# Relation stage of a graph network kernel: the next matrix split over two chunks, rows copied ahead of the splits, half loads behind their own chunk's store

## The reference, cut to what matters

```python
seg = edge_type * n + dst                                  # 34 relations
agg = segment_sum(x[src], seg, num_segments=N_REL * n)
cnt = segment_sum(ones, seg, num_segments=N_REL * n)
mean = agg.reshape(N_REL, n, -1) / maximum(cnt, 1.0).reshape(N_REL, n, 1)
h1 = einsum('rni,rio->no', mean, W_rel) + x @ W_root + b_rgcn
```

## Time and profile before

| | |
|---|---|
| median of three runs | 2671.55 us (2663.07 to 2681.05) |
| span of the profiled execution, which is all that is given of its own time | 2698.0 us |
| PE busy | 2339.2 us (87%) |
| DVE busy | 1509.4 us (56%) |
| ACT busy | 1065.7 us (39%) |
| POOL busy | 955.5 us (35%) |
| relation stage, in the span | about 590 us to 1610 us |

### The profile page before, as it was taken

How to read it: one execution, slowest core, us unless ns; L and a number is a source line. 1 busy time by engine, 2 the same in 40 slices (tenths; PEclk the granted TensorE clock), 3 DMA queues, 4 the chain that set the end, 5 groups by cost and what they waited for, 6 DMA issues and landing times.

```text
span 2698.0 us, 50471 instructions
## 1 busy us (share of the span) xinstructions
PE 2339.2 (87%) x12981; PEld 2168.2 (80%) x13015; DVE 1509.4 (56%) x2625; ACT 1065.7 (39%) x1833; POOL 955.5 (35%) x1138
## 2 busy tenths in 40 slices
PE   3677798879999999999999996788698879978899
PEld 1355698869999999999999984567598879978899
DVE  6654478754444333443433337777636777678634
ACT  3211332323334333433433335555423355347421
POOL 4766100015565555555555547676300000000000
PEclk9999899989999999999999998999899989989999
DMA  6000105345555555565555547777602110011102
GB/s 218 7 0 0 44 11 219 117 157 192 183 196 179 189 194 171 186 196 185 180 181 194 184 152 253 238 229 218 212 12 81 37 42 0 12 47 58 59 12 104
DMA packets 121823, 347.21 MB, mean 129 GB/s; under 512 B 30391, under 2 KB 31371, under 8 KB 121717
## 3 DMA queue, kind: packets, MB, share of 16 engines
q1 hardware_dynamic: 79973, 219.37, 23.2%
q0 software_dynamic: 41808, 127.32, 16.1%
HBM read 258.18 MB, written 92.26 MB: 130 GB/s over the span
## 4 chain that ended last, share of the span: by engine, by line
PE 37%; DMA 19%; issue 18%; DVE 12%; SPq 6%; ACT 4%; DVEq 3%; POOL 1%; ACTq 1%; POOLq 0%; another core or an unknown queue 0%
PE ps L1585 17%; PE ps L1654 12%; DMA messages<-land 10%; DMA land<-in_L_gnn_W_rel 6%; PE ps L1720 4%; DMA land<-messages,stage 2%; PE ps L1576 2%; SPq L550 2%; PE ps L1794 1%; SPq L564 1%; DVE xw L1543 1%; DVE h_act L1154 1%; DVE land L1167 1%; DVE w_a L1065 1%; DVE land L1221 1%
## 5 line engine op out<-in xcount | busy, mean ns | idle before, releaser
L1585 PE MATMUL ps<-w_a,h_t 128*128 128x384 f32 x4968 | 921.2, 342 | 11.9 <-issue 7.3
L1585 PEld LDWEIGHTS ps<-w_a,h_t 128*128 128x128 f32 x4968 | 872.0, 191 | 24.3 <-issue 16.6
L1492 DVE TENSOR_TENSOR h_t<-ps,h_t 128x256 fp32r<-128x256 f32 x408 | 172.3, 423 | 583.7 <-ACT h_t L997 440.0
L1654 PE MATMUL ps<-xw,agg_w 128*128 128x384 f32 x2500 | 460.5, 344 | 35.9 <-DVE agg_w L1176 29.8
L1654 PEld LDWEIGHTS ps<-xw,agg_w 128*128 128x128 f32 x2500 | 447.9, 193 | 44.9 <-issue 39.1
L1585 PE MATMUL ps<-xw,h_t 128*128 128x384 f32 x2448 | 456.5, 343 | 2.2 <-DVE h_t L1492 2.0
L1585 PEld LDWEIGHTS ps<-xw,h_t 128*128 128x128 f32 x2448 | 432.8, 190 | 3.6 <-issue 3.4
L997 ACT ACTIVATE h_t<-ps 128x256 fp32r<-128x256 f32 x408 | 156.3, 384 | 536.0 <-PE ps L1585 354.5
L692 POOL DMA_INDIRECT stage<-slot_table,stage x171 | 180.2, 1054 | 211.0 <-DMA stage<-inv_table,stage 159.6
L1576 PE MATMUL ps<-ident,land 128*128 128x128 f32 x1176 | 167.2, 279 | 87.2 <-DVE land L1488 36.6
L786 POOL DMA_INDIRECT land<-messages,stage x184 | 213.4, 1160 | 81.0 <-issue 46.6
(11 more groups left out here) (226 smaller groups left out, 2238.1 us busy)
## 6 DMA issues: line engine op xcount, KB each, us to landing
land<-in_L_gnn_W_rel SPq DMA_DIRECT2D x198, 384.0 KB
messages<-land SPq DMA_DIRECT2D x136, 384.0 KB
land<-x_state SPq DMA_DIRECT2D x40, 384.0 KB, 3.1
messages<-land SPq DMA_DIRECT2D x9, 1536.0 KB, 17.0
land<-in_L_gnn_W SPq DMA_DIRECT2D x10, 1152.0 KB
x_state<-land SPq DMA_DIRECT2D x30, 384.0 KB, 2.3
adj<-x_state SPq DMA_DIRECT2D x10, 384.0 KB
h_act<-x_state SPq DMA_DIRECT2D x1, 3840.0 KB
```

The lines of the kernel that those rows point to most:

```text
L1492: dve.tensor_tensor(h_t[:, 1, 2 * g:2 * g + 2, :], turn_group(g).rearrange("p (k n) -> p k n", k=2), h_t[:, 0, 2 * g:2 * g + 2, :].bitcast ...
L1585: ins = pe.matmul(acc(h), h_t[:, a, k, :], w[:, b, k, h * HF:(h + 1) * HF], start=(k == 0 and a == 0 and b == 0), stop=(stop and k == KB - ...
L1654: ins = pe.matmul(ps[:, 2 + 2 * u + h, 0:wide], at, xw[:, c, b, h * HF:h * HF + wide], start=first, stop=last, skip_group_check=True)
```

## The change

Four things are edited in the relation stage.

1. SP: `next_matrix` becomes `next_half`, which loads the three blocks of one half, one after the other; each waits for the one before it. The first half stands behind the first chunk's store, the second half behind the second chunk's. Before the first relation both halves of matrix 1 are loaded in the same way.
2. ACT and DVE: three blocks of the next matrix are split in the first chunk and three in the second, one block after each high or low part. In `rel_out`'s place nothing changes but that the third block's split stands ahead of it.
3. DVE: `copy_rows` stands right behind the first `rel_low` of a chunk, in every chunk, ahead of the splits.
4. Each relation has at least three chunks instead of two. The largest number of chunks grows, and with it some index tables; `stage` and `ctl_low` are made smaller or moved.

```diff
-    CH = 2 * NR + (E - 1) // P
+    CH = 3 * NR + (E - 1) // P
...
-            def next_matrix(r, w):
-                sp.wait_ge(w_low, r * 2 + w_no["rel"] * 2)
+            def next_half(r, w, h):
+                sp.wait_ge(w_low, r * 2 + (w_no["rel"] * 2 - 1 + h))
                 sp.sem_inc(turn_taken, 1)
                 for k in range(3):
-                    for h in range(2):
-                        if k > 0:
-                            sp.wait_ge(w_land[h], r * 48 + (w_no["rel"] * 16 - 32 + k * 16))
-                            sp.sem_inc(turn_taken, 1)
-                        b = 3 * h + k
-                        sp.dma_start(w_raw[:, b:b + 1, :], w[:, b * P:(b + 1) * P, :].rearrange("a (k p) d -> p (a k) d", p=P))\
-                          .then_inc(w_land[h], 16)
+                    if k > 0:
+                        sp.wait_ge(w_land[h], r * 48 + (w_no["rel"] * 16 - 32 + k * 16))
+                        sp.sem_inc(turn_taken, 1)
+                    b = 3 * h + k
+                    sp.dma_start(w_raw[:, b:b + 1, :], w[:, b * P:(b + 1) * P, :].rearrange("a (k p) d -> p (a k) d", p=P))\
+                      .then_inc(w_land[h], 16)
...
-                store(c0, c0, base)
-                if w is not None:
-                    next_matrix(r + 2, w)
-                with sp.Fori(c0 + 1, c1) as c:
+                for h in range(2):
+                    store(c0 + h, c0, base)
+                    if w is not None:
+                        next_half(r + 2, w, h)
+                with sp.Fori(c0 + 2, c1) as c:
                     store(c, c0, base)
...
-                    for g in range(KG):
-                        rel_high(c0 + 1, g)
-                        if g < KG - 1:
-                            rel_split(r + 1, 1 - u, 2 * g)
-                    rel_out(c0)
-                    rel_split(r + 1, 1 - u, 4)
-                    with act.Fori(c0 + 1, c1) as c:
+                    for n in range(2):
+                        for g in range(KG):
+                            rel_high(c0 + (n + 1), g)
+                            rel_split(r + 1, 1 - u, KG * n + g)
+                        rel_out(c0 + n)
+                    with act.Fori(c0 + 2, c1) as c:
...
-                dve.tensor_scalar(size, size, 2.0, None, ALU.max).then_inc(K.dve, 1)
+                dve.tensor_scalar(size, size, 3.0, None, ALU.max).then_inc(K.dve, 1)
...
-                    for g in range(KG):
-                        rel_low(c0 + 1, g)
-                        if g < KG - 1:
-                            rel_split(r + 1, 1 - u, 2 * g)
-                    copy_rows(c0 + 2)
-                    rel_split(r + 1, 1 - u, 4)
-                    with dve.Fori(c0 + 1, c1) as c:
-                        for g in range(KG):
+                    for n in range(2):
+                        rel_low(c0 + (n + 1), 0)
+                        copy_rows(c0 + (n + 2))
+                        rel_split(r + 1, 1 - u, KG * n)
+                        for g in range(1, KG):
+                            rel_low(c0 + (n + 1), g)
+                            rel_split(r + 1, 1 - u, KG * n + g)
+                    with dve.Fori(c0 + 2, c1) as c:
+                        rel_low(c + 1, 0)
+                        copy_rows(c + 2)
+                        for g in range(1, KG):
                             rel_low(c + 1, g)
-                        copy_rows(c + 2)
```

More of the change, by code:

```diff
@@ L247, in gnn_stack @@
         edge_slot, edge_weight = keys[:, 0, :], keys[:, 1, :].bitcast(F32)
-        stage = sb("stage", [P, 32], I32)
+        stage = sb("stage", [P, 24], I32)
         chunk_pos = sb("chunk_pos", [1, CW], I32)
@@ L251, in gnn_stack @@
         ctl_rel = sb("ctl_rel", [1, NR + 2], I32)
-        ctl_half = sb("ctl_half", [1, 5], I32)
+        ctl_half = sb("ctl_half", [1, 6], I32)
         ctl_quad = sb("ctl_quad", [1, NT + 1], I32)
         ctl_col = sb("ctl_col", [1, NT], I32)
-        ctl_low = sb("ctl_low", [1, 1], I32)
+        ctl_low = ctl_half[:, 5:6]
         deg = sb("deg", [P, NT], F32)
@@ L569, in relation @@
                 base = sp.value_load(ctl_base[0:1, ds(r, 1)], min_val=0, max_val=E)
-                store(c0, c0, base)
-                if w is not None:
-                    next_matrix(r + 2, w)
-                with sp.Fori(c0 + 1, c1) as c:
+                for h in range(2):
[3 more added lines that the diff above has]
+                with sp.Fori(c0 + 2, c1) as c:
                     store(c, c0, base)
             sp.wait_ge(K.dve, K.ctl)
-            next_matrix(1, w_rel[1:2, :, :])
+            for h in range(2):
+                next_half(1, w_rel[1:2, :, :], h)
             with sp.Fori(0, NR - 2) as r:
@@ L980, in _, with rel_split @@
             act.wait_ge(G["L0b"].mm, 2 * G["L0b"].last)
[L982 to L986, removed]
+            def rel_split(r, slot, p):
+                act.wait_ge(w_land[p // 3], r * 48 + (w_no["rel"] * 16 + 16))
+                act.activation(w_slot[slot][:, 0, p, :], w_raw[:, p, :], ACT.Copy).then_inc(R.whigh, 1)
             def rel_out(c):
@@ L1360, in _ @@
             dve.wait_ge(C.deg_max, 2)
-            dve.tensor_scalar(ctl_low[:], small[0:1, 5, 0:1], float(HIGH_EXACT), None, ALU.is_gt).then_inc(C.low_ctl, 1)
+            dve.tensor_scalar(ctl_low, small[0:1, 5, 0:1], float(HIGH_EXACT), None, ALU.is_gt).then_inc(C.low_ctl, 1)
             dve.sem_inc(F.ofree, 2)
@@ L1493, in rel_low, with rel_split @@
                                   h_t[:, 0, 2 * g:2 * g + 2, :].bitcast(F32), ALU.subtract).then_inc(R.low, 1)
-            def rel_split(r, slot, first):
+            def rel_split(r, slot, p):
                 w = w_slot[slot]
[L1498 to L1502, removed]
+                dve.wait_ge(R.whigh, r * KB + (p + 1 - KB))
+                ins = dve.tensor_tensor(w[:, 1, p, :], w_raw[:, p, :], w[:, 0, p, :].bitcast(F32), ALU.subtract)
+                if p % 3 == 2:
+                    ins.then_inc(w_low, 1)
             dve.wait_ge(R.ready, 1)
```

## The result

The kernel after takes 2825.9 us (2822.25 to 2828.65, four runs), the kernel before 2667.31 us (2653.54 to 2681.05, four runs, three of them those of the time before). The ratio is 1.0563, with a 95% interval of 1.052 to 1.0606: slower by 5.6%, some 159 us.

The account below looks back on a forecast made before the run. The prediction took SP's serial chain of waited DMAs as the bound: 33 relations x 4.0 us, less 8 at the end, is 124 us, scaled to 123, on 2671.55, about 2795 us (range 2710 to 2865, chance 0.80).

Parts of the forecast that it names:

- The bound: Relation stage: SP's chain of waited DMAs sets the pace at 29.84 us a relation, against PE's 28.0.
- The term: SP's loads by halves: four single waited loads instead of two rounds of pairs, 4.0 us more a relation.
- 4L + 2S + 3.34: SP's time from a relation's first load to its third store's landing after the change, forecast at 23.3 us.
- L: Time from a lone matrix load's issue to its landing on SP, between 2.9 and 3.8 us, taken as 3.2.
- S: Time of a store issued 1.06 us behind a load on SP, between 2.32 and 4.97 us, taken as 3.6.
- The 19.05 us: SP's stretch from first load to third store's landing in one relation of the kernel before (938.55 to 957.60).
- The ends: Loads before the first relation, about 20 us instead of 10.84, just covered; at the end PE's lead gives back about 8.
- The terms put at nothing: Early copy, splits over two chunks and larger tables: each costed at no change in time.
- What was late next: ACT's `rel_out` waits longest at a relation's first chunk; one PE stall of 3 to 6 us a relation.
- PE becomes the bound: Rival: quick lone loads put SP's cycle under PE's 28.0 us, 50 us faster, 2621 us; chance 0.08.
- Pairing bought nothing: Rival: two loads in flight on SP take twice one load, so no change, 2672 us; chance 0.07.
- Collisions: Rival: gathers meet most lone loads, about 8 us more a relation, 2925 us; beyond 2865 us has chance 0.05.

Follow-up runs that it names:

- the second profile of before: The kernel before, unchanged, run and profiled once more beside the follow-up kernels: 2670.39 us in one run.
- the pairs behind the second store: The kernel after, but SP loads the whole next matrix two loads at a time behind the second store: 2652.48 us, ratio to before 0.9908.
- the pairs with free look-ups: The kernel after, matrix loaded two loads at a time behind the second store, POOL's look-ups not waiting for each other: 2676.16 us, 0.9924 of before.

## Why the prediction was right

**The bound.** "A queue that waits for nothing but its own DMAs sets its own pace" held. SP's edit alone gives 1.0511 of the 1.0563, the early copy alone changes nothing that counts, other orders of the loads with the same copies and splits move the time from 0.9908 to 1.0959 of before.

**The term.** 4L + 2S + 3.34 was forecast at 23.3 us with L = 3.2 and S = 3.6. In the relation shown L is 3.69, 3.2, 3.1 and 3.06, mean 3.26, and S is 4.84 and 4.39. That makes 4 x 3.26 + 2 x 4.62 + 3.34 = 25.6, and the trace has 25.5. Over relations 1 to 29, SP's issue times, less the 0.21, 0.35 or 0.88 us that pass from a landing to the next issue, give 3.2 for L and 4.3 for S in the mean, and 24.7 us for the stretch. So L was right; S, taken as the middle of its two ends, was 0.7 us too small, and with it the sum 1.4 us a relation. The estimate of 2.9 us from the Trainium skill's anatomy of one DMA ("DMA: Bandwidth & Descriptors", a section on DMAs that GpSimd issues, while SP issues these) lies below that mean; 14 of the 116 waited loads were quicker than it, the quickest 2.7 us.

**Why the cycle still came near.** Forecast 4.0 us more a relation, measured 34.28 - 29.84 = 4.44, though the sum was 1.4 us too low. A second error offset most of that. The 19.05 us that the sum was set against are those of a quick relation (28.20 us, the mean is 29.84). By the same issue times the stretch is 20.1 us in the mean before, 19.7 in the second profile of before, and only 0.3 of that difference had been taken off for scatter. The links that stay hardly changed: they are 0.1 us shorter a relation, 0.4 against the second profile. So the mechanism and L were right; that the cycle came out within half a microsecond is in part luck, two errors of about one microsecond with opposite signs.

**The ends.** The loads ahead of the stage were covered, as forecast: from first load to first store 21.0 us (564.70 to 585.70), 20.8 before and 19.1 in its second profile. The whole stage grew by 1166.2 - 1023.5 = 142.7 us, or 150.0 against the second profile of before; 124 was forecast. The end gave back 33 x 4.44 - 142.7, about 4 us instead of 8, and nothing against the second profile (33 x 4.55 - 150.0).

**The terms put at nothing.** The early copy alone made the kernel before some 12 us faster (0.9955), and the edits beside SP's made after slower than SP's edit alone by a difference that the intervals don't tell from none. Both are small beside 159 us.

**The sum.** 2795 forecast, 2825.9 measured, inside 2710 to 2865. Of the 31 us, some 19 to 26 are the stage's. The rest wasn't traced; the median of before itself moved by 4 us.

**What was late next.** The longest waits of `rel_out` are at a relation's first chunk, as said (7.40 us), but there is a second place, the last chunk of the relation before (5.47 us), so PE has two stalls a relation (1.97 and 3.39 us) and not one. PE's share came out at 87% (forecast towards 85%). As forecast they don't add to SP's cycle.

**The rivals.** "PE becomes the bound" needed L under 2.4; the quickest load took 2.7. Its time, 2621 us, was approached only by the kernel that waits neither for its loads nor for look-ups, 2637.85. "Pairing bought nothing" is refuted by the pairs behind the second store. "Collisions" was right about S and wrong about L.

Left open: whether and why the other edits cost 0.76 us a relation on top of SP's, and why, for the pairs with free look-ups, what lies outside the stage took longer, so that the shorter cycle didn't show in the time.

## What to carry to other kernels

A queue that waits for each DMA before the next is an engine like any other: add its round trips up for one turn of the loop and set the sum beside the busiest engine's. PE busy for 96% of a stage doesn't show that PE bounds it; a list of waits in which the queue waits only for its own DMAs shows that the queue does. Before two transfers in flight are made into one after the other, price the round trips that come into the open; before all waits are taken out, look for another serial chain of small DMAs that the burst will stand in front of.

## What the runs showed that was not expected

Three chains of this stage lie within two and a half us of each other in the kernel before: SP's 29.8 us a relation, PE's 28.0, and POOL's 27.4, an estimate (29.84 less POOL's waits for copies, 80.4 us in 1000). With the waits between loads gone, POOL's look-ups waited up to 6.5 us behind bursts of three loads, and the cycle went to 30.3 us; with free look-ups it went to 28.1. So SP's waits had a use, which the kernel before doesn't tell: they kept the way clear for POOL. And a store right behind one load (4.3 us in the mean) takes almost as long as one behind two (5.1 us in the mean before, 4.7 in its second profile).
